# Projection of the graph values in two column halves, its weights in the query weights' place, and minima by pairs of heads from one count load

## What is computed

```python
xn = _layernorm(x, axis=-1)
xp = (x @ W).reshape(N, H, C)                  # x is xn; N 3125, H 4, C 256, D_IN 1024
a_src = jnp.einsum('nhc,hc->nh', xp, att_src)
a_dst = jnp.einsum('nhc,hc->nh', xp, att_dst)
src = jnp.concatenate([edge_index[0], loops])  # E 50000 edges and one loop for each node
e = jax.nn.leaky_relu(a_src[src] + a_dst[dst], NEG_SLOPE)
m = jax.ops.segment_max(e, dst, num_segments=N)
ee = jnp.exp(e - m[dst])
z = jax.ops.segment_sum(ee, dst, num_segments=N)
alpha = ee / z[dst]
out = jax.ops.segment_sum(xp[src] * alpha[:, :, None], dst, num_segments=N)
x = x + relu(out + bias) + mix(xn)             # mix: linear attention, 16 heads
x = x + ffn(_layernorm(x))                     # 1024 to 512 to 1024, piecewise linear gelu
```

## Time and profile before

| what | us |
|---|---|
| runs shown: median (lowest to highest) | 3538.54 (3536.8 to 3544.18) |
| profiled execution, its own time | 3533.52 |
| its span, first to last instruction | 3531.3 |
| TensorE matmuls busy | 3182.0 (90%) |
| VectorE busy | 2687.9 (76%) |
| ScalarE busy | 1249.1 (35%) |
| GpSimd busy | 1006.1 (28%) |
| mean granted TensorE clock | 0.955 |

### The profile page before, as it was taken

One profiled execution on the slowest core, in us unless ns is written; L12 is line 12 of the kernel. 1 busy time (PEld: TensorE's weight loads), 2 busy tenths in 40 slices (PEclk: granted clock), 3 DMA queues, 4 the chain that ended last, 5 costly groups with the idle time before them and its releaser, 6 DMA issues. The chain is left out here.

```text
span 3531.3 us, 44602 instructions
## 1 busy us (share of the span) xinstructions
PE 3182.0 (90%) x14812; PEld 2604.9 (74%) x14812; DVE 2687.9 (76%) x4763; ACT 1249.1 (35%) x1587; POOL 1006.1 (28%) x697
## 2 busy tenths in 40 slices
PE   6899999969999994999289999988988997799998
PEld 5678888848888883777178888877777886677776
DVE  5567676757777783454789889988988985888886
ACT  2111111121111111000256667656656743454544
POOL 1257773027776776675000000000000010000000
PEclk8999999989999997999699999999999999899999
DMA  7932322143444444322556985896697564322221
GB/s 264 365 73 53 70 53 69 47 143 76 88 93 87 88 87 92 58 45 47 149 139 172 264 230 157 230 250 173 173 249 210 157 181 130 106 70 87 70 87 41
DMA packets 327044, 461.02 MB, mean 131 GB/s; under 512 B 198006, under 2 KB 202202, under 8 KB 326934
## 3 DMA queue, kind: packets, MB, share of 16 engines
q1 hardware_dynamic: 139028, 381.48, 37.4%
q0 software_dynamic: 184656, 65.68, 10.4%
q10 hardware_dynamic: 3250, 12.50, 1.0%
HBM read 367.66 MB, written 90.80 MB: 130 GB/s over the span
## 5 line engine op out<-in xcount | busy, mean ns | idle before, releaser
L1309 PE MATMUL G_acc<-values,G_weight 125*125 125x257 f32 x5000 | 1119.1, 386 | 89.2 <-DVE G_weight L1238 50.1
L1309 PEld LDWEIGHTS G_acc<-values,G_weight 125*125 125x125 f32 x5000 | 949.1, 191 | 248.3 <-DVE G_weight L1238 58.4
L318 POOL DMA_INDIRECT counts<-E_twins_now,E_cells_now x400 | 864.4, 2161 | 380.8 <-issue 255.5
L1128 ACT ACTIVATE G_weight<-G_weight,G_asrc_slope 125x750 f32<-125x750 f32 (+1 forms) x400 | 377.1, 943 | 230.9 <-DVE G_weight L1229 230.7
L1229 DVE SCALAR_TENSOR_TENSOR G_weight<-G_rows,G_asrc_most 125x750 f32<-125x750 f32 (+1 forms) x400 | 411.0, 1028 | 48.0 <-PE G_acc L1309 34.4
L1197 DVE SCALAR_TENSOR_TENSOR G_least<-G_absent,asrc_all,G_least 125x750 f32<-125x750 bf16 (+1 forms) x384 | 391.8, 1030 | 72.0 <-ACT G_absent L1102 71.2
L1238 DVE SCALAR_TENSOR_TENSOR G_weight<-G_weight,G_count 125x750 f32<-125x750 f32 (+1 forms) x400 | 387.0, 968 | 3.0 <-ACT G_weight L1128 2.8
L1072 POOL DMA_DIRECT2D shifts<-G_shiftsT x16 | 8.3, 520 | 1119.5 <-ACT G_shiftsT L1134 1119.5
L219 PE MATMUL V_v_ps<-V_w,V_xT 128*125 128x512 f32 x1200 | 281.6, 397 | 46.5 <-DVE V_xT L243 46.5
L219 PEld LDWEIGHTS V_v_ps<-V_w,V_xT 128*125 128x125 f32 x1200 | 224.3, 187 | 103.8 <-DVE V_xT L243 46.9
L219 PE MATMUL Q_q_ps<-Q_wq,Q_xT 128*125 128x512 f32 x1200 | 288.3, 399 | 11.9 <-DVE Q_xT L243 11.9
(11 more groups left out here) (170 smaller groups left out, 3403.7 us busy)
## 6 DMA issues: line engine op xcount, KB each, us to landing
G_count<-counts SPq DMA_DIRECT2D x300, 328.1 KB
G_next_count<-counts SPq DMA_DIRECT2D x150, 328.1 KB
G_count<-counts SPq DMA_DIRECT2D x100, 382.8 KB
counts<-K_zeros POOLq DMA_DIRECT2D x50, 763.5 KB, 8.5
xnT<-K_xT_whole SPq DMA_DIRECT2D x25, 500.0 KB, 6.3
Q_xT_whole<-xnT SPq DMA_DIRECT2D x25, 500.0 KB, 3.6
V_xT_whole<-xnT SPq DMA_DIRECT2D x25, 500.0 KB, 3.5
gat<-G_sums POOLq DMA_DIRECT2D x100, 125.0 KB, 6.7
```

The source lines that it names most:

```text
L318: nc.gpsimd.indirect_dma_start(out=counts_cells, out_offset=bass.IndirectOffsetOnAxis(ap=self.cells_now[:, slot, c:c + 1], axis=0), in_=se ...
L1128: nc.scalar.activation(here, here, ACT.Exp, bias=asrc_slope[:, u % H, j:j + 1]).then_inc(exp_ready, 1)
L1309: m = nc.tensor.matmul(acc[0:T, t, 0:CW], weight[:, k % RING, t * T:(t + 1) * T], values[:, j, h, :], start=(j == 0), stop=(j == NT - 1))
```

## The change

- `whole` is one place for the weights of K, of the queries and of the values, laid out in two halves of 512 columns. `whole_plain` is the same memory seen as plain floats. The turned rows (`xT`, `xT_whole`) also get one place for all stages. In G the ring buffers lie in this memory.
- In Q, ScalarE issues the eight loads of W as soon as the last query projection is done, and splits it there together with VectorE.
- V runs over 50 half passes: 25 tiles for columns 0 to 511, then 25 for the rest. From the second half on SP loads counts, ScalarE masks, and VectorE takes the minima of units 0 and 1; they are turned at pass 48, and unit 0's row is broadcast before V ends.
- For this all scatters must have landed at pass 25: 20 units in K, 2 in QP, 23 in Q, 5 in V.
- In G one extra count load and one mask serve the two heads of a pair. Both minima are taken one after the other. The first 20 steps take two minima each, later steps one; pair `p` is complete 20 steps before its first unit.
- A copy of the turned Wo in QP is shared between ScalarE and VectorE.

```diff
-UNITS_K, UNITS_Q = 15, 24
+UNITS_K, UNITS_P, UNITS_Q = 20, 2, 23
...
+            @block.gpsimd
+            def _(pool):
+                edges.scatter(pool, a["counts_cells"], UNITS_K, UNITS_K + UNITS_P)
...
+                if not fixed(g, 0, NT - 2):
+                    act.wait_ge(q_done, NT)
+                    for b in range(KB):
+                        act.dma_start(a["whole_plain"][:, :, 1, b, :], a["gnn_w"][b * 128:(b + 1) * 128, :].rearrange("p (i n) -> p i n", i=2)).then_inc(w_loaded[b], 16)
+                    act.wait_ge(xn_loaded, NT * 16 + 16)
+                    high(nc, xT[:, 0, :, :], xT_whole[:, :, :]).then_inc(xT_high, 1)
                 act.wait_ge(q_turned, g + 1)
                 high(nc, qT[:, 0, :, :], trq[:, :, 0:T]).then_inc(qT_high, 1)
             over_tiles(act, body, **ONE)
+            for b in range(KB):
+                act.wait_ge(w_loaded[b], 16)
+                high(nc, wq[:, :, 0, b, :], a["whole_plain"][:, :, 1, b, :]).then_inc(w_high, 1)
...
+            for b in range(KB):
+                dve.wait_ge(w_high, b + 1)
+                low(nc, wq[:, :, 1, b, :], a["whole_plain"][:, :, 1, b, :], wq[:, :, 0, b, :]).then_inc(w_low, 1)
             finish(NT - 1)
...
+    passes = nearest.loaded[0:2]
+    WHOLE = 2 * NT
+    TURN = NT + 23
+
+    def passes_of(q):
+
+        done_by = [(NT * max(0, min(22, q + i - NT))) // 22 for i in range(2)]
+        return range(*done_by)
...
+            for q in range(WHOLE):
+                if 1 <= q < WHOLE - 1:
+                    sp.wait_ge(xT_low, q)
+                    load_turned(q + 1)
+                if q == NT:
+                    sp.wait_ge(done, NT)
+                    load_terms(1)
+                    sp.wait_ge(edges.scattered, 16 * NCH)
+                for n in passes_of(q):
+                    nearest.load(sp, ring, n, 0, passes)
...
+                if q >= 4:
+                    pe.wait_ge(summed, q - 3)
+                here = xT[:, q % 2, :, :, :]
+                product(nc, v_ps[0:T, q % 4, :], lambda s, b: here[:, s, b, :], lambda m, b: w[:, q // NT, m, b, :], KB).then_inc(done, 1)
...
+    LEAD = 20
+    FIRST, LAST = 2 * NT, 2 * NT * PAIRS
...
+    def least_by(k):
+
+        return min(LAST, FIRST + k + min(k, LEAD))
+
+    def absences_by(k):
+
+        return min(LAST, least_by(k + 2) + 1) // 2
+
+    def fold_at(u):
+
+        return 1 if u == 1 else 2 * NT * (u // 2) - LEAD + 11 * (u % 2)
...
-            for j in range(NT):
-                load_next(j, 0, j)
-                if j < RING:
-                    load_count(j)
+            for k in range(RING):
+                load_count(k)
+            for n in range(NT, absences_by(0)):
+                nearest.load(sp, next_count, n, NT, next_loaded)
             for k in range(STEPS):
-                u, j = k // NT, k % NT
-                if u + 2 < UN and not own_counts(u):
-                    load_next(nexts_before(u) + j, u + 2, j)
+                for n in range(absences_by(k), absences_by(k + 1)):
+                    nearest.load(sp, next_count, n, NT, next_loaded)
                 if k + RING < STEPS:
                     load_count(k + RING)
...
-                if u + 2 < UN:
-                    nearest(u + 2, j, absents_before(u) + j, least_steps(u + 2) + j)
+                for m in range(least_by(k), least_by(k + 1)):
+                    nearest.step(dve, absent, m)
```

580 lines of the change are left out of this document (292 added, 288 removed).

## The result

| | before | after |
|---|---|---|
| median of 4 runs, us (lowest to highest) | 3540.93 (3536.8 to 3544.18) | 3461.92 (3460.39 to 3469.26) |
| span of the profiled execution | 3531.3 | 3459.1 |
| mean granted TensorE clock | 0.955 | 0.972 |

The ratio is 0.9782, with a 95% interval from 0.9766 to 0.9798: 79 us less. The prediction was 3408, so 54 us of the gain that it promised are missing, though the direction holds and 3461.92 lies at the very edge of the range (3378 to 3462). The span fell by 72.2 where the sum had said 127.7. The stretches show in which stages.

A forecast was written before the change was run, and what follows sets the result against it. TensorE filled the projection stages; scatters and weight loading held a border, VectorE or doubled count loads the attention pairs. Terms +3, -38.7, +17.5, -61.5, -48 sum to -127.7 from 3533.5: 3405.8, stated as 3408 us, range 3378 to 3462.

The forecast's parts named there:

- Terms 1 and 2: Stages before values: moved scatter units cost +3 us; weights loaded and split inside the query stage save 38.7.
- Term 3: Values stage: fifty half passes instead of 25 whole ones, single plain row buffer, 299 us instead of 281.5, +17.5.
- Rival B: Values stage, second half: row loads slow beside count loads, loop 7.7 us, half 193, execution 3450; chance 0.14.
- sign that the prediction had named for a wrong forecast: Values stage: first-half passes over 6 us; attention loop: units 6 and 7 still differing from 4 and 5.
- Term 4: Start of the attention stage: first minima gone, 23 us instead of 84.4 to its first matmul, -61.5.
- Term 5: Attention loop: 20 earlier minimum steps +21 us, fewer extra count loads -73, stalls +4; together -48.
- the forecast's pairs: Attention loop: pair 1 goes like pair 0, 169.2 to 161.2 us; pairs 2 to 5 go like pair 6.
- The share of 0.85: Attention loop, DMA engines: 75 count loads a pair need 115 us of 135.

The follow-up runs named there:

- run 4: The changed kernel with each extra attention-loop count load from unit 4 on issued again into an unread place; 3524.28 us, loop 1256.4 instead of 1184.8.
- run 1: The changed kernel with a second buffer for the plain turned rows in the values stage; 3435.53 us, that stage 297.4 instead of 318.6.

## Why the prediction was right or wrong

**Terms 1 and 2, the front: the number right, the last engine wrong.** The query stage began at 772.8 on average against 774.3, the values stage at 1377.5 against 1376.5. The weights' loads, copies and subtractions are hidden beside the last mixer product, as said. That GpSimd would end near 1364 was wrong in all ten executions: it ended between 1366.6 and 1380.5, and in six of them last. These six reached the first value matmul at 1380.0 on average and the other four at 1373.6, so that the average met the forecast is in part luck. The estimate took the mean of 25.7 a unit and left no room for scatters of 6 us or gaps beside the 4 MB weight load.

**Term 3, the passes: the mechanism right, the size off by 19.3 us.** "The loop is: landing 3.5 us (median), ScalarE 1.04, VectorE 1.20, together 5.75" was the right ring. The step that failed came after it: "In the first half this fits under 5.63, since ScalarE's copy lies beside the dot products". That compares VectorE's 3.2 us with the matmuls, and the ring does not fit: 5.75 is over 5.63, and measured it was 5.80 a pass. The first half took 150.3 us, 6.0 over its forecast of 144.3. In the second half the ring took 6.1 to 6.9 in most passes instead of 5.85 (3.8 to 4.6 from issue to copy instead of 3.5), the three passes with four minimum steps 7.25 instead of 7.7, and the border had been counted at nothing, since only the scatters' wait was looked at there and not the three broadcasts beside it. It cost 7.3 us: 5.9 of standstill, the rest because the pass behind it ran at a lower granted clock. The half missed 155 (with the turning) by 13. Rival B had the right place, the second half, and the right sign, with too high a price (193 us). One more buffer took 21.2 us off, the border's loads 6.2: 27.4 in all, more than the 19.3 missed. Neither sign that the prediction had named for a wrong forecast showed: the passes of the first half stayed under 6 us, and units 6 and 7 went like 4 and 5. Both were set too wide to find this.

**Term 4, the opening: right.** 21.4 against 23, and ScalarE did wait for the masks' loads; the masks were made at 1718.69 and 1720.03. Part of it was a cost of order, though, and not of the loads: 8.6 us could be had back by another order, and the first matmul then came 10.4 us after the last value matmul.

**Term 5, the loop: the gain was there, and 4 us of stalls were 48.** That fewer loads would make the slow pairs quick was right, and run 4 shows it by undoing it. The extra 20 minimum steps cost what was said (unit 0: 101.3). Against the forecast's pairs the measured ones are, from pair 0 on: 2.1 less, 6.4 less, then 11.2, 8.9, 9.0 and 9.7 more; the last two together are 5.1 more. The step that failed is "I allow 4 us of stalls". VectorE's waits for loads, direct or by the exponential, are 47.8 us in units 2 to 13. The share of 0.85 was about right (0.80 to 0.83), but a mean share says nothing of the stretches in which a broadcast of 732 KB passes on the same engines with the loads of both rings. Why that broadcast takes 15.5 us stays open: the larger one of the seven-tile units took 5.9 to 10.4, as told at the end, and no run tried another layout for it. The pairs with their own counts had an average share of 0.6, and their 135.3 was taken for a loop at 0.85. On the other side pair 1 was taken to go like pair 0 (161.2), though the minima made in it are six tiles wide. VectorE's work in it was already in the earlier trace rows, 148.98 us, and 154.8 was the result: TensorE's 153.4 sets it.

## What to carry to other kernels

Where one buffer is loaded, split and freed in a ring, add the ring up, from issue to issue, and compare it with the pace of the engine it feeds before calling it hidden; a tenth of a microsecond over the pace is paid in every pass. When doubled loads are spread evenly over all stages, the stages that were quick at a low DMA share do not stay as they were: look for the large transfers that will now collide with them, and for the instruction in order behind the one that waits for a late load. A mean DMA share does not show either. Look also at how long each shape of such a transfer took before the change: the smaller one was the slower one here.

## What the runs showed of the hardware

The row broadcast, 732 KB from a few rows in HBM to 125 partitions, took 15.5 us at the median of twelve to land beside the count loads, in the changed kernel. The row of the seven-tile units is larger and took 9.0:

```profile
whole_plain<-shifts POOLq DMA_DIRECT2D x12, 732.4 KB, 15.5
...
whole_plain<-shifts POOLq DMA_DIRECT2D x4, 854.5 KB, 9.0
```

The page "DMA: Bandwidth & Descriptors" of the Trainium skill ("Anatomy of one DMA — SWDGE (gpsimd) path") fits a transfer issued by GpSimd as 2.0 us and the bytes divided by 436e3, an estimate of 3.7 us for 732 KB. The row is four times that.

Traffic beside it is only a part of this. The 854.5 KB row issued at 1698.95 landed after 5.9 us with no other queue's packets under way, and the one issued at 1953.96 after 10.0 us in a pair with a DMA share of 0.83. The 732 KB rows took 14.2 us even in the last pair (share 0.54), 14.0 to 17.4 in all, and ten of the twelve took 18.2 to 21.0 with the doubled loads of run 4. What sets the two shapes apart is the place that they fill: a row's two parts are 875 floats apart there, so 875 floats each fill it without a gap and 750 do not. The trace has 144 packets of GpSimd's queue for the first, 125 of them of 7000 bytes, and 416 for the second, 125 of 6000 bytes and 275 of 8. Before the change it was the same: 6.2 to 9.9 us for the larger row, 13.4 to 17.4 for the smaller. That the gap and the small packets make the difference is likely and not shown; a row place 750 floats wide would try it.

The engines moved 264 GB/s at a share of 0.99, with count rows of 3 to 3.5 KB as most of the traffic. From 95 to 165 us of the changed kernel, where most of the traffic is GpSimd's writing of zeros to `counts`, they moved 359 GB/s at a share of 0.93. So a rate alone does not tell how full they are.

After a standstill of 4.45 and 5.9 us in the values stage the granted clock was 0.66 (run 1, 1540 to 1548) and 0.76 (changed kernel, 1551 to 1558), and one pass took 8.2 and 7.3 us instead of 5.6.

The stages before the first value matmul vary by 9 to 12 us from execution to execution with the same code (first query matmul 769.1 to 778.0, first value matmul 1371.4 to 1383.7, ten executions), while the last two units of the loop take 65.0 and 65.2 us in all eleven executions. A gain of a few microseconds behind a stage with scatters has to be read inside its own stage.
